# The recurrence of a mixed model: order of the waits before four instructions, and of VectorE's sums

## The reference, cut to what matters

```python
def step(h, x_t):
    hid = jnp.broadcast_to(h[:, None, :], (Bn, Sn, Hn))
    combined = jnp.concatenate([hid, enc_hiddens], axis=2)
    score = jnp.tanh(jnp.einsum('bsk,kh->bsh', combined, W_att))
    score = jnp.einsum('bsh,h->bs', score, V_att[:, 0])
    attn = jax.nn.softmax(score, axis=-1)
    context = jnp.einsum('bs,bsh->bh', attn, enc_hiddens)
    inp = jnp.concatenate([x_t, context], axis=1)
    gz, gr, gh = jnp.split(inp @ Wi + b, 3, axis=1)
    rz, rr, rh = jnp.split(h @ Uh, 3, axis=1)
    z = jax.nn.sigmoid(gz + rz)
    r = jax.nn.sigmoid(gr + rr)
    hh = jnp.tanh(gh + r * rh)
    h_new = z * h + (1.0 - z) * hh
    return (h_new, h_new)
_, outs = jax.lax.scan(step, last_hidden, jnp.swapaxes(dec_seq, 0, 1))
```

## Time and profile before

| | us |
|---|---|
| time, median of 3 runs | 4559.13 (4556.88 to 4564.08) |
| the profiled execution | 4555.23 |
| its span, first to last instruction | 4553.4 |

### The profile page before, as it was taken

One profiled execution on the slowest core, in us unless ns is written; L12 is line 12 of the kernel. 1 busy time (PEld: TensorE's weight loads), 2 busy tenths in 40 slices (PEclk: granted clock), 3 DMA queues, 4 the chain that ended last, 5 costly groups with the idle time before them and its releaser, 6 DMA issues. The chain is left out here.

```text
span 4553.4 us, 70928 instructions
## 1 busy us (share of the span) xinstructions
PE 3742.8 (82%) x20207; PEld 2115.2 (46%) x20268; DVE 2845.1 (62%) x13500; ACT 2234.7 (49%) x6560; POOL 707.3 (16%) x2308
## 2 busy tenths in 40 slices
PE   7877777777777777777799999678888888888868
PEld 2366666666666666666533234322333333333222
DVE  3467777777777777777654554546666666666534
ACT  5345555555555555555533334214555555555423
POOL 0312222222222222222230000300000001000002
PEclk8999999999999999999999999768888888888879
DMA  0100000000000000000101000011111111111000
GB/s 9 56 1 2 1 1 1 1 2 1 1 1 1 1 2 1 1 1 1 36 1 37 1 1 1 22 56 45 45 58 45 57 58 45 58 53 51 31 30 5
DMA packets 48789, 93.75 MB, mean 21 GB/s; under 512 B 11296, under 2 KB 31792, under 8 KB 48144
## 3 DMA queue, kind: packets, MB, share of 16 engines
q1 hardware_dynamic: 48400, 89.22, 6.1%
HBM read 72.88 MB, written 15.39 MB: 19 GB/s over the span
## 5 line engine op out<-in xcount | busy, mean ns | idle before, releaser
L926 PE MATMUL ps<-g_dh,w_p 128*128 128x77 f32 x2032 | 454.1, 305 | 445.0 <-DVE g_dh L1021 444.7
L2257 ACT ACTIVATE t_ex<-ps 128x1024 f32<-128x1024 f32 (+1 forms) x480 | 471.8, 1021 | 571.2 <-PE ps L2204 557.6
L934 PE MATMUL ps<-g_dh,w_p 128*128 128x128 f32 x4064 | 668.2, 286 | 0.0
L993 DVE SCALAR_TENSOR_TENSOR g_used<-g_encg,g_e 128x77 f32<-128x77 f32 x3072 | 626.4, 229 | 1.9 <-issue 1.4
L926 PEld LDWEIGHTS ps<-g_dh,w_p 128*128 128x128 f32 x2032 | 303.9, 189 | 638.3 <-DVE g_dh L1021 637.6
L2352 DVE TENSOR_REDUCE t_ncol<-ps 128x1 f32<-128x512 f32 x768 | 486.2, 682 | 154.0 <-PE ps L2177 153.4
L934 PEld LDWEIGHTS ps<-g_dh,w_p 128*128 128x128 f32 x4064 | 540.1, 193 | 0.0
L962 ACT ACTIVATE g_th<-ps 128x77 f32<-128x77 f32 x1024 | 241.5, 236 | 606.7 <-PE ps L926 606.7
L1021 DVE SCALAR_TENSOR_TENSOR g_dh<-g_hh,g_hist,g_omz 128x1 f32<-128x1 f32 x1024 | 224.3, 219 | 386.1 <-ACT g_hh L975 385.7
L975 ACT ACTIVATE g_hh<-ps,g_hin,g_tzr 128x1 f32<-128x1 f32 x1024 | 359.9, 351 | 213.7 <-DVE g_hin L997 213.4
L938 PE MATMUL ps<-g_dh,g_uhh 128*128 128x129 f32 x2032 | 439.0, 298 | 0.0
(11 more groups left out here) (486 smaller groups left out, 5731.3 us busy)
## 6 DMA issues: line engine op xcount, KB each, us to landing
t_qst<-t_turn_q SPq DMA_DIRECT2D x288, 96.0 KB
t_kst<-t_turn_k SPq DMA_DIRECT2D x144, 96.0 KB
t_turn_q<-t_part SPq DMA_DIRECT2D x24, 384.0 KB, 2.5
t_turn_k<-t_part SPq DMA_DIRECT2D x12, 384.0 KB, 3.3
t_wf<-in_t_wf SPq DMA_DIRECT2D x6, 514.5 KB, 5.5
m_experts<-in_experts SPq DMA_DIRECT2D x1, 3072.0 KB, 12.9
t_wa<-in_t_wa SPq DMA_DIRECT2D x6, 448.0 KB, 3.6
t_wx<-in_t_wx SPq DMA_DIRECT2D x6, 448.0 KB, 4.3
```

Source lines behind the costliest of these rows:

```text
L926: M(att[c], w["att_h"], moved(c, t, S), start=False, stop=True, skip_group_check=True).then_inc(*st.sem("att", c))
L934: return M(gates[c][:, g], w["uh"][:, g * D:(g + 1) * D], moved(c, t, SPAN), start=False, stop=False, skip_group_check=True)
L993: V.scalar_tensor_tensor(out=used[:, c, g], in0=encg[:, g, c], scalar=1.0, in1=e[:, c], op0=ALU.mult, op1=ALU.mult, accum_out=mac[:, c, g: ...
L2257: A(ex[0:kw, slot[pf, c, l, n]], ps[0:kw, at:at + 2], ACT.Exp, scale=SCALE).then_inc(*st.sem(f"{pf}e{n}", c))
```

## The change

Two kinds of edits, all in the loop of the recurrence. In four places two waits ahead of an instruction swap their places: at the exponential, at the candidate, at the gates' sum `zr`, and at the update; the update's third wait, for `h` of the last step, goes (POOL makes `omz` of a token after the `h` of the token before, in its queue's order, so the wait for `omz` includes it). And on DVE the candidate's weighted sum `hm` moves ahead of `zr`, so that the sums stand in the order r, z, hm, with the names in `Steps` to match. No computation changes.

```diff
         st = Steps(k, "g", 2, pe="att rough score gates", act="tanh exp tzr cand",
-                   dve="top sinv r z zr hm in dh", pool="omz h")
+                   dve="top sinv r z hm zr in dh", pool="omz h")
...
                 def exp(c, t):
+                    act.wait_ge(*st.at("top", c, t))
                     act.wait_ge(*st.at("score", c, t))
-                    act.wait_ge(*st.at("top", c, t))
                     A(e[:, c], score[c], ACT.Exp, bias=ntop[:, c:c + 1], accum_out=esum[:, c:c + 1])\
                         .then_inc(*st.sem("exp", c))
 
                 def candidate(c, t):
                     act.wait_ge(*st.at("zr", c, t))
                     A(tzr[:, c], zr[:, c], ACT.Tanh, scale=0.5).then_inc(*st.sem("tzr", c))
+                    act.wait_ge(*st.at("tzr", c, t))
                     act.wait_ge(*st.at("in", c, t))
-                    act.wait_ge(*st.at("tzr", c, t))
...
                     weigh("r", 1, c)
                     weigh("z", 0, c)
+                    weigh("hm", 2, c)
+                    dve.wait_ge(*st.at("z", c, t))
                     dve.wait_ge(*st.at("gates", c, t))
-                    dve.wait_ge(*st.at("z", c, t))
                     fma("zr", c, zr[:, c], mac[:, c, 0:2], sinv[:, c:c + 1], gates[c][:, 0:2, t % SPAN])
-                    weigh("hm", 2, c)
                     dve.wait_ge(*st.at("hm", c, t))
...
                 def update(c, t):
-                    if t:
-                        dve.wait_ge(*st.at("h", c, t - 1))
+                    dve.wait_ge(*st.at("cand", c, t))
                     dve.wait_ge(*st.at("omz", c, t))
-                    dve.wait_ge(*st.at("cand", c, t))
```

## The result

The changed kernel takes 4344.9 us (median of 4 runs, 4341.2 to 4355.8), against 4558.4 us before; the ratio is 0.9535, with a 95% interval of 0.9518 to 0.9551. That is 213.5 us less. Of the 230 us forecast this is 93%, and 4344.9 lies in the range of 4300 to 4395.

What follows compares the result with a forecast made beforehand. Latency in two rings, within 0.05 us of each other, was taken as the bound. One sequence's ring falls from 3.86 to 3.41 us: 0.225 us per half step, times 1,024 = 230 us, giving 4329 us; range 4300 to 4395.

Steps and rivals of the forecast that it cites:

- ring of one sequence: One sequence's loop from `dh` to its next `dh`: forecast 3.41 instead of 3.86 us, half a step 1.705.
- ring across: Loop through both sequences, the exponential queued on ACT behind the other's candidate: forecast 1.67 us per half step.
- What a wait costs by its place: Wait satisfied last: 0.03 to 0.04 us if the instruction carries it, 0.09 to 0.14 as a separate instruction.
- Update: At `dh` on DVE: carried wait on the candidate costs 0.04 instead of 0.14; candidate to `dh` 0.39 us.
- Sums: On DVE: `hm` 0.14 behind z, `zr` at z + 0.28 instead of z + 0.36, 0.08 us less.
- Irregular intervals: Longer intervals of the recurrence, 28 us of 2002.5, left as they are; half gone at the range's low end.
- Exponential: On ACT: with `top` carried and the score separate, it starts 1.60 us after `dh` instead of 1.69.
- `omz`: POOL's product for the update: allows `dh` at `zr` + 0.84, the candidate's route 0.87; hidden by 0.03 us only.
- Queued behind the waits: On DVE the wait for `omz` holds back the other sequence's reciprocal and sums; reciprocal wanted 0.37 us after `dh`.
- The rivals: Other outcomes: `hm` holds `zr` (chance 0.05), wait places worth nothing (0.09), `omz` last at the update (0.17), slower (0.02).
- the slower rival: At the update, `omz` seen over 0.59 us after its end; at 0.7, 56 us more, 4615 us; chance 0.02.
- Its signs: Expected in the new profile: `dh` intervals 1.70 to 1.72 us, `zr` 0.28 behind z, `dh` 0.04 behind the candidate.

Runs made afterwards that it cites:

- e1: Changed kernel with every wait as in the kernel before, so only the new order of the sums: 4464.3 us, ratio 0.9794.
- e2: Changed kernel with DVE's sums in the old order (r, z, zr, hm), so only the new wait places: 4520.9 us, ratio 0.9918.
- e3: Changed kernel with the update's three waits as before, including the one for `h`: 4394.5 us, ratio 0.9646.
- e4: Changed kernel with the candidate's two waits as before (`in` carried, `tzr` separate): 4387.9 us, ratio 0.9622.
- e5: Changed kernel with the two waits of `zr` as before (`gates` carried, z separate): 4377.7 us, ratio 0.9605.
- e6: Changed kernel with the exponential's two waits as before (score carried, `top` separate): 4353.2 us, ratio 0.9544.
- e7: Changed kernel with the reciprocal of the sum of exponentials moved from DVE to POOL, as a power of -1: 4608.5 us, ratio 1.0108.
- e8: Changed kernel with DVE's sums in the old order and the candidate's waits as before: 4460.7 us, ratio 0.9783.
- e9: Changed kernel with DVE's reciprocal moved behind sums r and z, `zr` carrying the wait for it: 4350.3 us, ratio 0.954.

## Why the prediction was right

**What bounds it.** Two rings of latency, within 0.05 us of each other. Right: the rhythm came within 0.01 us of the larger of the two rings each time. The table takes each stretch of a ring as its median over the half steps of that run. For `dh` to exponential it takes 1.61, what it is where the other ring does not hold it, and 1.63 where the exponential's waits stand as before.

| run | ring of one sequence, half | ring across | rhythm |
|---|---|---|---|
| before | 1.90 | 1.93 | 1.930 |
| changed | 1.73 | 1.72 | 1.733 |
| e1 | 1.84 | 1.83 | 1.847 |
| e2 | 1.83 | 1.91 | 1.908 |
| e3 | 1.78 | 1.72 | 1.782 |
| e4 | 1.76 | 1.78 | 1.775 |
| e5 | 1.75 | 1.76 | 1.758 |
| e6 | 1.74 | 1.72 | 1.742 |
| e7 | 1.86 | 1.97 | 1.966 |
| e8 | 1.80 | 1.85 | 1.850 |

**What a wait costs by its place.** Right, and now shown with the same instructions in both places: `tzr` to candidate 0.10 against 0.04 (e4, 43 us), z to `zr` 0.36 against 0.32 (e5, 33 us), candidate to update 0.13 against 0.03 (e3, 50 us, of which some 15 are the third condition's). Against the repetition of the changed kernel each of the three is 5 us less.

The prediction only argued that the queue goes on once a separate wait is over. The traces have records of the wait instructions, which the timelines leave out, and they show it. L1010 is the wait ahead of `zr` in the step of the earlier trace rows, and L1011 the one in the changed kernel's step above (count, duration in ns, first and last start):

```profile
L1010 DVEq EVENT_SEMAPHORE  x1: 21/21/21, 1003.9 to 1003.9; - x1
```

```profile
L1011 DVEq EVENT_SEMAPHORE  x1: 21/21/21, 1013.0 to 1013.0; - x1
```

Before, this was the wait for z. It starts at 1003.86, 0.04 after the sum is written (1003.82), lasts 0.02, and `zr` starts 0.06 after its end: together the 0.12. After, it is the wait for `gates`. It ends at 1012.98, before r starts and 0.50 before `zr`, so the queue is long past it. On ACT the same parts are 0.03, 0.02 and 0.05 (e4, `tzr` to candidate). Where a separate wait is satisfied last, these parts hold within 0.01 us in at least nine tenths of the half steps. The Trainium skill (Perfetto Trace Analysis, Identifying Dependency Chains) says that an instruction that waits on several engines may get separate instructions ahead of it with the other conditions. That agrees with the built order here; it names no price.

**Update.** 0.39 forecast, 0.38 measured (1013.96, 1014.34). The third condition that went has a price of its own where it stands in a wait that is satisfied last. These are the update's separate waits of the whole run, L1020 before and L1018 in the changed kernel:

```profile
L1020 DVEq EVENT_SEMAPHORE  x1024: 21/50/50, 257.4 to 2259.9; - x171
```

```profile
L1018 DVEq EVENT_SEMAPHORE  x1024: 21/21/21, 256.0 to 2044.5; - x171
```

With two conditions the wait lasts 50 ns, with one, as in the first step of each sequence before, 21 ns. That is the difference between the 0.14 and the 0.11 that the prediction read, and in the changed kernel the wait for `omz` is hidden.

**Sums.** This is the term that was mis-sized. The prediction put `hm` 0.14 behind z and `zr` 0.14 behind `hm`, by the distance from r to z. That pair is the exception: the 0.14 belongs to the sum right behind the reciprocal, whichever it is (e9), and every other sum takes 0.16. So z to `zr` is 0.32 and not 0.28. The row was there: in the earlier trace rows the write of z's sum starts 0.16 after z (1003.58, 1003.74), and the next instruction starts no earlier than such a write, as 1013.32 shows twice. That is 0.04 of the 0.06 us by which the ring is longer than forecast (3.47 for 3.41); the exponential, at 1.62 instead of 1.60, is 0.02. In the rhythm 1.733 for 1.705 us, times 1,024, is 29 us less gain than forecast.

**Irregular intervals.** Left as they are in the sum; they shrank by 12 us, which gives back some of those 29: 230 - 29 + 12 = 213, for 213.5 measured. That the sum came so near owes that much to luck, since the two misses have opposite signs and the second stands in the prediction only at the low end of its range. Without it the kernel would be at 4357 us, still in the range.

**Exponential.** 1.60 forecast, 1.62 measured in the step shown and 1.61 as the median. The prediction held the ring across to be 0.035 below the other, 1.67 against 1.705; measured it is 1.72 against 1.73. In the half step shown the exponential comes 0.28 behind the other sequence's candidate (1012.21, 1012.49) and waits for the score. In 47% of the half steps it comes at the least distance, 0.25, and waits for ACT itself.

**`omz`.** Hidden by the forecast 0.03: it ends at 1014.20, a separate wait of 0.11 gives 1014.31, `dh` starts at 1014.34. A faster route of the candidate would meet it next. A version with a later `omz` was not tried.

**Queued behind the waits.** The prediction had the reciprocal wanted 0.37 after the other sequence's `dh` (2.08 - 1.71), but its 2.08 goes with the exponential at 1.64. With its own 1.60 it is 0.34. In the changed kernel the other sequence's `dh` starts at 1012.59 and the reciprocal at 1012.93, so it is 0.34. Nothing hangs on it.

**The rivals.** `zr` is not held behind `hm`: 0.16, while `hm`'s record lasts 0.23. The Trainium skill (VectorE: DVE Perf Modes, The DRAIN you can't avoid) says that an operation starts only once the pipe is empty, but adds in the same paragraph that one which is not held starts earlier. The prediction weighed only the first sentence; the 0.14 and 0.16 go with the second. The place of a wait is worth something (e4, e5 and, less the third condition, e3). `omz` did not become last. A POOL product behind a separate wait is seen 0.14 after its end (e7), far from the 0.59 from which the slower rival would have decided.

**Its signs.** The forecast's intervals of 1.70 to 1.72 us and `zr` 0.28 behind z did not come: they are 1.733 (1.748 with the irregular ones) and 0.32, the first for the most part and the second wholly by the term above. The others came, and none of the signs of being wrong did.

**Open.** Why fewer long intervals remain with the new places of the waits (28.0 us before, 21.0 in e1, 11.6 and 11.1 in e2 and e8). Beside the six at the 128th tokens, most of them begin with one instruction that starts 0.1 to 0.35 us later than usual behind the work or the instruction ahead of it (looked at in the half steps 100 to 270 of both traces). In the changed kernel `dh` starts at 686.51, 0.35 behind its candidate's end instead of 0.03. The same happens again every 128 half steps; the cause is not shown.

## What to carry to other kernels

In a loop bound by latency, look at each instruction with two waits: which one is satisfied last, and does the instruction carry it? The right place depends on the order of the work around it, so the places have to be gone through again after each reordering; here one swap lost 60 us with the old order and gained 43 with the new. Work that fills a wait costs its slot once the wait is made short, and the slot is read from the distance between starts of the very same pair of instructions.

## What the runs showed of the hardware

- A weighted sum over 77 columns followed by the write of its result takes 0.16 us of DVE before the next instruction starts, though its record lasts 0.23. Right behind the reciprocal it takes 0.14 or 0.15 (r in the changed kernel, `hm` in e9); r without the reciprocal ahead of it takes 0.16 (e9).
- POOL's power on 128x1 takes 0.60 us, where its multiply and add takes 0.19.
- A wait in a separate instruction costs ACT 0.10 us from the end of the work waited for (e2, e4), whether that work was DVE's or its own. On DVE it costs 0.10 to 0.12 with one condition in it, for its own work (before, e5) and ACT's (first steps of before and e3), and 0.13 to 0.14 with two, for ACT's (before, e3) and POOL's (e7). Carried by the instruction, a wait costs either engine 0.03 to 0.04.
- A separate wait on DVE has a record of 21 ns with one condition and 50 ns with two (before, e3, e7). Where it is satisfied last, it starts 0.04 us after the end of the work waited for, and the instruction behind it 0.05 to 0.06 us after the wait's end.
